# Last batch of a folded cross-attention: order of running sums, reciprocals in quarters, and the order of four divisions

## The reference

```
q = rmsnorm(layernorm(x) @ Wq) ; k = rmsnorm(ctx @ Wk) ; v = ctx @ Wv      # per head, D = 128
attn = softmax(q k^T / sqrt(D))                                            # over the 1601 keys
x = x + concat_heads(attn @ v) @ Wo
```

## Time and profile before

| what | value |
|---|---|
| median of three runs | 1493.97 us |
| profiled execution: its own time | 1493.47 us |
| its span | 1491.5 us |
| TensorE busy | 1471.7 us, 99% |
| VectorE busy | 1238.7 us, 83% |
| ScalarE busy | 986.7 us, 66% |
| mean granted TensorE clock | 0.999 |

### The profile page before, as it was taken

The page is one execution under the profiler, slowest core; times in us unless marked ns, Lnnn a source line. Parts: engine busy times, 40 slices in busy tenths (PEclk is TensorE's granted clock), DMA queues, the critical chain, the costliest instruction groups (busy, mean ns, idle before and its releaser), DMA issues.

```text
span 1491.5 us, 22107 instructions
## 1 busy us (share of the span) xinstructions
PE 1471.7 (99%) x6913; PEld 1194.8 (80%) x6949; DVE 1238.7 (83%) x1942; ACT 986.7 (66%) x3719; POOL 165.5 (11%) x120
## 2 busy tenths in 40 slices
PE   8999999999999999999999999999999999999998
PEld 7777778888888888888888888888888877788787
DVE  8758888989888988899889988998898899777643
ACT  5676776776776767667766766776677666556432
POOL 3210000002000200020011002000200210123342
PEclk9999999999999999999999999999999999999999
DMA  6542221211121121112111111121011133841000
GB/s 202 162 138 71 78 64 53 67 36 57 60 61 43 55 61 56 46 54 65 55 40 62 57 55 45 56 62 48 25 56 43 34 107 105 266 185 59 1 1 29
DMA packets 86660, 105.21 MB, mean 71 GB/s; under 512 B 7304, under 2 KB 67728, under 8 KB 85392
## 3 DMA queue, kind: packets, MB, share of 16 engines
q1 hardware_dynamic: 79248, 96.46, 20.9%
q10 hardware_dynamic: 7296, 7.34, 1.5%
HBM read 81.24 MB, written 22.54 MB: 70 GB/s over the span
## 4 chain that ended last, share of the span: by engine, by line
PE 85%; DVE 9%; issue 2%; ACT 2%; DMA 0%; POOL 0%; SPq 0%; ACTq 0%; DVEq 0%; POOLq 0%
PE ps L36 27%; PE ps L37 25%; PE ps L38 25%; DVE ring L1172 3%; PE ps L934 2%; PE ps L935 2%; DVE p_lo L42 2%; PE ps L952 1%; PE ps L953 1%; ACT ps L1741 1%; PE ps L807 1%; DVE ring L1143 0%; ACT recip L1778 0%; DMA wq_raw<-in_wq 0%; PE ps L564 0%
## 5 line engine op out<-in xcount | busy, mean ns | idle before, releaser
L1741 ACT ACTIVATE ps<-ps 123x128 f32<-123x128 f32 (+1 forms) x1248 | 326.2, 261 | 141.6 <-PE ps L38 141.4
L36 PE MATMUL ps<-wk_hi,cT_hi 128*128 128x512 f32 x832 | 329.0, 395 | 1.6 <-ACT sq L1735 1.4
L37 PE MATMUL ps<-wk_lo,cT_hi 128*128 128x512 f32 x832 | 325.9, 392 | 0.0
L38 PE MATMUL ps<-wk_hi,cT_lo 128*128 128x512 f32 x832 | 323.9, 389 | 0.0
L1741 ACT ACTIVATION_READ_ACCUMULATOR ps<-ps 123x1 f32 (+1 forms) x1248 | 232.0, 186 | 0.0
L36 PEld LDWEIGHTS ps<-wk_hi,cT_hi 128*128 128x128 f32 x832 | 156.3, 188 | 38.9 <-issue 3.6
L38 PEld LDWEIGHTS ps<-wk_hi,cT_lo 128*128 128x128 f32 x832 | 156.3, 188 | 34.1
L37 PEld LDWEIGHTS ps<-wk_lo,cT_hi 128*128 128x128 f32 x832 | 156.6, 188 | 32.3
L36 PE MATMUL ps<-p_hi,cn_hi 123*128 123x512 f32 (+1 forms) x400 | 164.7, 412 | 0.0
L36 PE MATMUL ps<-fq_hi,cT_hi 128*128 128x512 f32 x416 | 162.2, 390 | 0.6 <-DVE w_scale L1260 0.4
L38 PE MATMUL ps<-fq_hi,cT_lo 128*128 128x512 f32 x416 | 161.9, 389 | 0.0
(11 more groups left out here) (241 smaller groups left out, 2702.9 us busy)
## 6 DMA issues: line engine op xcount, KB each, us to landing
cT_raw<-in_ctxT SPq DMA_DIRECT2D x96, 128.0 KB, 3.6
cn_raw<-in_ctx SPq DMA_DIRECT2D x88, 123.0 KB
w_raw<-in_wguT SPq DMA_DIRECT2D x32, 256.0 KB, 2.7
qk_scratch<-folded ACTq DMA_DIRECT2D x8, 896.0 KB, 4.2
fq_raw<-qk_scratch SPq DMA_DIRECT2D x14, 512.0 KB, 3.8
pc_scratch<-pc_out SPq DMA_DIRECT2D x7, 1024.0 KB, 4.2
ternary_scratch<-w_out SPq DMA_DIRECT2D x48, 128.0 KB, 1.7
w_raw<-in_wpT SPq DMA_DIRECT2D x16, 256.0 KB, 2.6
```

The source lines that it names most:

```text
L36: pe.matmul(dst, l_hi, r_hi, start=first, stop=False)
L37: pe.matmul(dst, l_hi, r_lo, start=False, stop=False)
L38: return pe.matmul(dst, l_lo, r_hi, start=False, stop=last)
L1741: done = act.activation(head, head, ACT.Square, accum_out=k_sum[0:n, i, g * GH + h:g * GH + h + 1])
```

## The change

Four edits, all behind the last batch's scores:

1. In the hand-written list two `track_sum` stand later, behind the low parts of later tiles, and `rescale_context(1)` stands behind `low_cn(second + 2)`.
2. `last_refine` works on quarters (256 columns, four heads): quarter 0 before `add_parts(0)`, quarter 1 behind `oT_lo` of head 0, quarters 2 and 3 behind `low_pc(2)`. TensorE waits for the PSUM reads of both banks: outputs m = 2 for a count of 17, m = 3 for a count of 21.
3. `divide_parts(1)` (heads 5 to 8) moves from head 2 to head 1's turn, ahead of the divisions 2 and 3; these move from the end of head 1's turn to the end of head 2's, behind `low_pc(4)`.
4. ScalarE's `high_pc(4)` waits for two divisions instead of four, SyncE waits for all four instead of three.

```diff
-                if heads[0] == 0 and O_BANK + m == PART_SUM_BANK + 1:
-                    pe.wait_ge(sum_refined, 2 * (B - 1) + 3)
+                if heads[0] == 0 and O_BANK + m >= PART_SUM_BANK:
+
+                    pe.wait_ge(sum_refined, 2 * (B - 1) + 4 * (O_BANK + m - PART_SUM_BANK) + 3)
...
-            def last_refine(half):
+            def last_refine(g):
 
-                first, hh = 2 * (B - 1) + 2 * half, slice(half * BANK, (half + 1) * BANK)
-                dve.wait_ge(sum_guessed, first + 2)
+                first, half = 2 * (B - 1) + 2 * g, g // 2
+                cols, in_half = slice(g * width, (g + 1) * width), slice(g % 2 * width, (g % 2 + 1) * width)
+                dve.wait_ge(sum_guessed, 2 * (B - 1) + 2 * half + 2)
                 dve.wait_ge(sum_spread, B + half)
-                dve.tensor_tensor(run_sum[:, hh], bank(PART_SUM_BANK + half), recip[:, hh], ALU.mult).then_inc(
-                    sum_refined, 1)
+                dve.tensor_tensor(run_sum[:, cols], bank(PART_SUM_BANK + half)[:, in_half], recip[:, cols],
+                                  ALU.mult).then_inc(sum_refined, 1)
...
             numerator_lo(second - 2)
-            track_sum(second - 3)
-            track_sum(second - 2)
             subtract_max(second)
             numerator_lo(second - 1)
             subtract_max(second + 1)
             factor_log()
             numerator_lo(second)
             subtract_max(second + 2)
-            rescale_context(1)
+            track_sum(second - 3)
             numerator_lo(second + 1)
             low_cn(second + 2)
+            rescale_context(1)
             subtract_max(second + 3)
+            track_sum(second - 2)
             track_sum(second - 1)
             numerator_lo(second + 2)
...
                 if head == 0:
                     last_refine(1)
-                if head == 2:
+                if head == 1:
                     divide_parts(1)
                 if head + 2 < H:
                     low_head_weights(head + 2)
                     low_pc(head + 2)
-                if head == 1:
+                if head == 0:
+                    last_refine(2)
+                    last_refine(3)
+                if head == 2:
                     divide_parts(2)
                     divide_parts(3)
...
                 if head == GH:
-                    act.wait_ge(evacuated, evacuations(B - 1))
+                    act.wait_ge(evacuated, KC * (B - 1) + 2)
...
-                sp.wait_ge(evacuated, evacuations(b) if b < B - 1 else KC * b + 3)
+                sp.wait_ge(evacuated, evacuations(b))
...
-            sp.wait_ge(evacuated, KC * (B - 1) + 3)
+            sp.wait_ge(evacuated, evacuations(B - 1))
```

More of the change, by code:

```diff
@@ L1222, in sum_refine @@
                 dve.wait_ge(sum_refined, 2 * b + 2)
-            def last_refine(half):
-                first, hh = 2 * (B - 1) + 2 * half, slice(half * BANK, (half + 1) * BANK)
-                dve.wait_ge(sum_guessed, first + 2)
+            def last_refine(g):
+                first, half = 2 * (B - 1) + 2 * g, g // 2
+                cols, in_half = slice(g * width, (g + 1) * width), slice(g % 2 * width, (g % 2 + 1) * width)
+                dve.wait_ge(sum_guessed, 2 * (B - 1) + 2 * half + 2)
                 dve.wait_ge(sum_spread, B + half)
-                dve.tensor_tensor(run_sum[:, hh], bank(PART_SUM_BANK + half), recip[:, hh], ALU.mult).then_inc(
-                    sum_refined, 1)
+                dve.tensor_tensor(run_sum[:, cols], bank(PART_SUM_BANK + half)[:, in_half], recip[:, cols],
+                                  ALU.mult).then_inc(sum_refined, 1)
                 dve.wait_ge(sum_refined, first + 1)
-                dve.scalar_tensor_tensor(out=recip[:, hh], in0=run_sum[:, hh], scalar=2.0, in1=recip[:, hh],
+                dve.scalar_tensor_tensor(out=recip[:, cols], in0=run_sum[:, cols], scalar=2.0, in1=recip[:, cols],
                                          op0=ALU.subtract, op1=ALU.mult, reverse0=True).then_inc(sum_refined, 1)
```

## The result

The changed kernel takes **1501.18 us** (median of six runs, 1500.1 to 1501.77) against 1493.85 us for the kernel before (six runs, 1492.95 to 1494.78): 7.3 us more, ratio 1.0048 with a 95% interval of 1.0035 to 1.0061. Slower was forecast, at 1499.6 us in a range of 1496.6 to 1502.6 us. The profiled execution took 1501.05 us with a span of 1499.3 us, 7.8 us more than the span of before.

A forecast was written before the change was run, and what follows sets the result against it. TensorE was taken as the bound (85% of the span), with value(8) waiting on a late load. Profiled 1493.47 us plus 4.1 us delay plus 2.0 us low clock gave 1499.6 us, range 1496.6 to 1502.6 us.

The forecast's parts named there:

- The chain divisions 2 and 3, store, load, pc_hi(8), value(8): VectorE through SyncE and ScalarE to TensorE: already late by 0.65 us, and 4.1 us later with the change.
- Release to landing: SyncE's release to the landing of the load of sums: 18.6 us, with nothing in it absorbing the delay.
- The steps behind the landing: pc_hi(8), pc_lo(8) and TensorE's start of value(8) behind the load: 2.05 us, as in the profile before.
- gains ahead of value(8): TensorE's earlier gains or losses (0.28, 0.54, 0.5, 0.44 us): covered by the wait for the load, counting nothing.
- Release later: SyncE's release by divisions 2 and 3 on VectorE: 4.1 us later, at 1271.8 instead of 1267.70.
- the last rival: New 2.2 us gaps also lower the clock and delay division 3, or later weights share bandwidth: 1501.5 us, chance 0.15.
- Clock: TensorE's granted clock falls behind the 5.2 us gap before value(8): 2.0 us, with bounds of nothing and 3.4 us.
- the forecast's own 1498.3 to 1500.9: Whole kernel: the time range in us for delayed value(8) plus low clock, with a chance of 0.52.
- the moved gap before tile second+2: TensorE behind the sums: waits 2.2 us for a low part, starting at 1242.40 instead of 1242.68.
- value(4), forecast 0.4 us earlier: TensorE at value(4): pc_hi(4) no longer waits, so it starts 0.44 us earlier, at about 1270.7.
- no change: Store and load path has unseen slack and shrinks, value(8) late by under 3 us: 1495.5 us, chance 0.13.
- faster: The load lands early enough to cost nothing and TensorE keeps full clock at 1259: 1490.4 us, chance 0.04.

The follow-up runs named there:

- b: Kernel before with only the order of the four divisions and the waits on them changed; 1500.05 us.
- a: Changed kernel with divisions 2 and 3 put back at the end of head 1's turn; 1495.81 us.
- k: Changed kernel with SyncE issuing the weights of heads 9 to 12 ahead of its wait for the divisions, and three bias loads behind the load of sums; 1493.78 us.
- c: Kernel before with only the running sums and rescale_context(1) moved; 1493.92 us.
- d: Kernel before with only the refinement in quarters and its waits on TensorE; 1494.79 us.
- i: Changed kernel with 36 useless identity turns on TensorE right ahead of value(8), to fill the gap; 1498.8 us.
- e: Changed kernel with 16 useless identity turns on TensorE right ahead of value(8), to fill the gap; 1500.6 us.
- j: Changed kernel with the three bias loads moved behind the load of the sums, weights still behind the store; 1497.43 us.
- f: Changed kernel with SyncE issuing the weights of heads 9 to 12 ahead of its wait for the divisions; 1496.30 us.
- g: Kernel before with moved sums, new division order and waits, weights ahead of the divisions' wait, biases behind the sums' load, no quarters; 1491.80 us.

## Why the prediction was right, and where it was not

**Right.** The chain divisions 2 and 3, store, load, pc_hi(8), value(8) was named as the one that decides, from its 0.65 us of lateness. Run b makes it alone, a undoes it, k shortens it. Release to landing was said to be rigid, 18.6 us: with SyncE's list as it was it took 18.0 (a), 18.3 (after, c), 18.6 (d), 18.8 (i) and 19.0 us (b, e). The steps behind the landing took 2.05 us as before. That gains ahead of value(8) count nothing was shown by b, where value(4) is 1.35 us earlier and the gap before value(8) only longer. TensorE was in fact ready for value(8) at 1288.55, not at 1287.3, so the gap was 4.40 us instead of 5.2; the load decided all the same.

**Sizes that were off.** Both terms of the sum were too small, 4.1 and 2.0 us against 4.60 and 2.81 in the profile; none made up for another.
- Release later: 4.1 us by the sum, 4.90 in the trace. I wrote that VectorE waits for nothing on the way and that oT_hi(2) is 0.9 us early. It was late: VectorE waited 0.53 us for it (row at 1268.54). The new 2 us wait of the fourth output lowered the clock (windows from 1262 to 1270), which I had only in the last rival, with 0.6 to 0.7 us for it. The stretch also lay 0.16 us later as a whole in this execution. The path behind the release was 0.3 us shorter, which makes 4.60 for value(8).
- Clock: 2.0 us taken, 2.81 measured by the trace, 1.86 by that of b, 2.4 by the medians of i and the changed kernel. I had priced it by a short low stretch in which TensorE partly waited; behind a 4.4 us gap it restarts low and stays low until about 1298.9.
- 1501.18 us lies above the forecast's own 1498.3 to 1500.9 and next to the last rival's 1501.5, which had a chance of 0.15; the range held it because it took that rival in. Of the rival's three parts one came in the profile, the wait of the fourth output with the low clock. The gap of the sums kept the clock there, but lowered it in e and i. The weights of heads 13 to 16 were issued 1.2 us behind the load instead of 5.4 and did not lengthen it: from its issue to pc_hi(8) it took 10.2 us, before 10.7.

**Wrong in place, without effect on the sum.** I put the moved gap before tile second+2, behind a late low part. It came earlier, at 1237.84, before the ones matmuls of tile second: they write PSUM banks 6 and 7, which rescale_context(1) must have read, and edit 1 moved that read back. I had followed the low parts and not this wait, and missed that a moved instruction also holds a bank. And value(4), forecast 0.4 us earlier, came at 1272.07, 0.95 us later than before, because of the low clock of the 2 us wait. It is covered by the load.

The rivals of no change and of faster did not come: the transfers did shrink by 0.3 us, far from the 3.1 us at which they would have decided.

## What to carry to other kernels

Before giving an engine a better order, look which of the moved instructions starts a transfer, and follow it to its reader; an operation that costs 1.3 us of VectorE can stand at the head of an 18 us path. What a DMA waits for belongs as early as possible, and what nobody needs soon belongs behind it in the queue: moving three bias loads behind the load and the weights well ahead of the store took 5 us off that path and turned a 7.3 us loss into none. And a long gap on TensorE is to be priced with its low clock behind it, here 4.6 us of delay and 2.8 us on top.

## What the runs showed of the hardware

- Three bias loads, 516 KB in all, ahead of a 512 KB store made store-to-load 6.7 us instead of 3.7 (after against j), more than the 1.5 MB of weights behind it did (5.6 in f).
- The length of a gap alone does not decide whether the clock falls. The gap of 1.82 to 1.86 us before the ones matmuls kept the full clock in four profiles (after, a, c, j) and lowered it in five (e, f, g, i, k), with 0.57 from 1238 to 1242 in e, f and i. The gap of 2.03 to 2.08 us before the fourth output lowered it in seven and kept it in k. Before value(8) the clock held behind 1.84 (j), 1.94 (f) and 3.37 us (e, partly filled) and fell with 4.40 (after) and 5.58 us (b). What decides stays open, and the timed runs of e, one program, lay 4.6 us apart.
- TensorE at the low level starts a matmul of 512 columns every 0.43 us against 0.23, and an identity turn of 128 columns takes 0.12 us at the full level.
